# Causal linear attention on one core: a tile of 128 tokens worked as two chunks of 64 in divided TensorE arrays

## The reference

```python
q = (x @ Wq.T) -> 16 heads of 128;  k, v = (x @ Wk.T), (x @ Wv.T) -> 4 heads of 128
q, k = rope(q), rope(k);  qf, kf = elu(q) + 1, elu(k) + 1      # each k, v head serves 4 q heads
def step(carry, inp):                                          # once for each of 1024 tokens
    state = state + k_s[..., :, None] * v_s[..., None, :]
    z = z + k_s
    num = einsum('bhe,bhed->bhd', q_s, state)
    den = einsum('bhe,bhe->bh', q_s, z)[..., None] + 1e-6
    return (state, z), num / den
out = out.transpose(...) @ Wo.T
```

## Time and profile before

| what | value |
|---|---|
| median of three runs | 1032.81 us (1032.09 to 1033.21) |
| profiled execution, its own time | 1031.37 us |
| its span in the trace | 1029.6 us |
| PE busy over the span | 976.8 us (95%) |
| DVE, ACT, POOL busy | 681.7, 332.3, 249.5 us |
| TensorE's granted clock, mean | 0.995 of full |

### The profile page before, as it was taken

The page is one execution under the profiler, slowest core; times in us unless marked ns, Lnnn a source line. Parts: engine busy times, 40 slices in busy tenths (PEclk is TensorE's granted clock), DMA queues, the critical chain, the costliest instruction groups (busy, mean ns, idle before and its releaser), DMA issues. The chain is left out here.

```text
span 1029.6 us, 15693 instructions
## 1 busy us (share of the span) xinstructions
PE 976.8 (95%) x5994; PEld 791.1 (77%) x5994; DVE 681.7 (66%) x1494; ACT 332.3 (32%) x604; POOL 249.5 (24%) x320
## 2 busy tenths in 40 slices
PE   5899999999999999999978999998999999999997
PEld 4688888888888888888856788885666667778875
DVE  6766766666766667666565977765676776476556
ACT  4343333433333343334313323221122232422220
POOL 2232312222212323122201010023334554211011
PEclk9999999999999999999998999999999999999999
DMA  9400000000000000000004000002455340000000
GB/s 297 142 1 1 1 1 1 1 1 1 1 1 1 1 1 2 1 1 1 1 21 137 1 1 1 1 1 42 124 115 113 92 84 22 1 16 16 11 21 20
DMA packets 33051, 33.37 MB, mean 32 GB/s; under 512 B 6857, under 2 KB 26834, under 8 KB 32978
## 3 DMA queue, kind: packets, MB, share of 16 engines
q1 hardware_dynamic: 32978, 32.38, 11.9%
HBM read 23.98 MB, written 8.13 MB: 31 GB/s over the span
## 5 line engine op out<-in xcount | busy, mean ns | idle before, releaser
L396 POOL TENSOR_TENSOR rope_sum<-rope_cos,rope_sin 128x512 f32<-128x512 f32 x80 | 115.0, 1437 | 257.0 <-DVE rope_sin L517 257.0
L432 ACT ACTIVATE rope_exp<-rope_sum 128x512 f32<-128x512 f32 x80 | 50.5, 631 | 205.2 <-POOL rope_sum L396 205.1
L786 PE MATMUL proj<-wo_sb,attn_out_t 128*128 128x256 f32 x512 | 113.2, 379 | 0.7 <-issue 0.7
L786 PEld LDWEIGHTS proj<-wo_sb,attn_out_t 128*128 128x128 f32 x512 | 96.1, 190 | 13.4 <-issue 0.9
L735 PE MATMUL num<-v_ones,score_masked 128*128 128x129 f32 x512 | 99.2, 275 | 5.9 <-DVE score_masked L575 5.9
L736 PE MATMUL num<-state,q_t 128*128 128x129 f32 x512 | 99.0, 275 | 0.0
L2052 DVE SCALAR_TENSOR_TENSOR m_acc<-m_expert,gates,m_acc 128x256 f32<-128x256 f32 x128 | 61.9, 484 | 46.3 <-PE m_expert L2101 39.9
L735 PEld LDWEIGHTS num<-v_ones,score_masked 128*128 128x128 f32 x512 | 82.1, 191 | 13.4 <-DVE score_masked L575 8.0
L514 DVE TENSOR_TENSOR rope_cos<-proj,cos_sb 128x512 f32<-128x512 f32 x80 | 55.3, 691 | 52.3 <-PE proj L689 52.3
L689 PE MATMUL proj<-w_hi,a_h_hi 128*128 128x512 f32 x192 | 79.0, 493 | 4.1 <-DVE w_lo L139 2.4
L736 PEld LDWEIGHTS num<-state,q_t 128*128 128x128 f32 x512 | 77.7, 192 | 0.0
(11 more groups left out here) (250 smaller groups left out, 1883.6 us busy)
## 6 DMA issues: line engine op xcount, KB each, us to landing
kv_scratch<-t_kv SPq DMA_DIRECT2D x16, 256.0 KB, 2.4
kv_rows<-kv_scratch SPq DMA_DIRECT2D x32, 128.0 KB, 3.7
a_stage<-in_wqkv SPq DMA_DIRECT2D x6, 512.0 KB, 5.3
wo_sb<-in_wo SPq DMA_DIRECT2D x1, 2048.0 KB, 9.6
a_stage<-in_wgu SPq DMA_DIRECT2D x4, 512.0 KB, 9.7
out<-x_sb SPq DMA_DIRECT2D x16, 128.0 KB, 1.7
u_scratch<-u_rows SPq DMA_DIRECT2D x28, 64.0 KB, 2.9
t_u<-u_scratch SPq DMA_DIRECT2D x14, 128.0 KB, 2.2
```

Of the source, the lines that this page charges most:

```text
L396: pool.tensor_tensor(y[:, parity], t1[:, parity], t2[:, parity], ALU.add).then_inc(s["y_done"], 1)
L786: mm = pe.matmul(proj[:, b, 0:D], o_t[:, i, :], wo[:, i, :], start=(i == 0), stop=(i == H - 1))
```

## The change

The tile's 128 tokens become two sides of 64. On TensorE:

- `scores(g)` is now two products, one for each side: 64 tokens of k (64 columns of the array) with the four heads' q of the same side (256 columns streamed). The two write partitions 0 to 63 and 64 to 127 of one bank. Scores between the second side and the first are no longer made.
- `numerators(g)` has, for each of two values of j, four products of 64 x 64 masked scores with `[v | 1]` of their side, in four quarters of the array, then four of 64 columns of q with a state, in two halves of the array. The first side takes `state`, the second takes `mid`.
- `mid` is the state at the tile's middle: `sums(..., slice(0, HP))`, four products over the first 64 tokens, stands behind `turn4(0)`, and DVE adds it to `state` at the head of its step. `mid` lies in the buffer `g_xn`, and has that name in the rows.
- The sums over all 128 tokens at the step's end stay, but are left out in the last chunk (steps 14 and 15), where nothing reads the state any more.
- The mask and the masking on DVE cover 256 columns in place of 512; ACT's copies of q and of the output put the two sides apart and together again; GpSimd makes the mask in two halves.

```diff
+HP = P // 2
-            causal = sb("causal", [P, P])
+            causal = sb("causal", [P, HP])
-            k_t, q_t = sb("k_t", [P, KVH, P]), sb("q_t", [P, KVH, REP * P])
+            k_t, q_t = sb("k_t", [P, KVH, P]), sb("q_t", [P, KVH, 2, REP, HP])
+            mid = self.g_xn[:].rearrange("p i d -> p (i d)")[:, 0:KVH * VW].rearrange("p (g w) -> p g w", w=VW)
+            def num_item(c, b, j):
+                return at(c, b, KVH + 2, j) - (1 if last(c, b) else 0)
...
                     for g in range(KVH):
-                        drain_turn(c, b, 1 + g, q_t[:, g], turn[:, bank(1 + g), :])
+                        drain_turn(c, b, 1 + g, q_t[:, g].rearrange("p k r t -> p r k t"),
+                                   turn[:, bank(1 + g), :].rearrange("p (r k t) -> p r k t", r=REP, k=2))
...
                     def masked(g):
                         dve.wait_ge(s["score_full"], at(c, b, KVH, g + 1))
-                        dve.tensor_tensor(am[:, g % 2].rearrange("p (r t) -> p r t", r=REP),
-                                          score[:, g % 2, :].rearrange("p (r t) -> p r t", r=REP),
-                                          causal[:].unsqueeze(1).broadcast_to([P, REP, P]),
+                        dve.tensor_tensor(am[:, g % 2, 0:REP * HP].rearrange("p (r t) -> p r t", r=REP),
+                                          score[:, g % 2, 0:REP * HP].rearrange("p (r t) -> p r t", r=REP),
+                                          causal[:].unsqueeze(1).broadcast_to([P, REP, HP]),
                                           ALU.mult).then_inc(s["score_free"], 1)
+                    def state_of(item, dst):
+                        dve.wait_ge(s["num_full"], item + 1)
+                        dve.tensor_tensor(dst.rearrange("p (k h) w -> p k (h w)", k=2), num[:, :, 0:2 * VW],
+                                          state[:, b].rearrange("p (k h) w -> p k (h w)", k=2),
+                                          ALU.add).then_inc(s["num_free"], 1)
...
+                    state_of(num_item(c, b, 0), mid)
                     if nxt:
                         split(at(c, b, 1, 2), nb, 2 + 1 + at(c, b, 10, 1))
...
-                        pe.matmul(score[:, g % 2, :], k_t[:, g, :], q_t[:, g, :], start=True, stop=True
-                                  ).then_inc(s["score_full"], 1)
+                        for side in range(2):
+                            rows = slice(side * HP, (side + 1) * HP)
+                            mm = pe.matmul(score[rows, g % 2, 0:REP * HP], k_t[:, g, rows],
+                                           q_t[:, g, side].rearrange("p r t -> p (r t)"), start=True, stop=True)
+                        mm.then_inc(s["score_full"], 1)
                     def numerators(g):
                         pe.wait_ge(s["score_free"], 2 + at(c, b, KVH, g + 1))
-                        pe.wait_ge(s["num_free"], at(c, b, KVH + 1, g + 1))
-                        for r in range(REP):
-                            dst = num[:, r // 2, (r % 2) * VW:(r % 2 + 1) * VW]
-                            pe.matmul(dst, am[:, g % 2, r * P:(r + 1) * P], v[:, b, g, :], start=True, stop=False)
-                            mm = pe.matmul(dst, q_t[:, g, r * P:(r + 1) * P], state[:, b, g, :], start=False, stop=True)
+                        pe.wait_ge(s["num_free"], num_item(c, b, 1 + g) + 1)
+                        for j in range(2):
+                            places = [(side, q, num[q * HP:(q + 1) * HP, side, j * VW:(j + 1) * VW], 2 * j + q)
+                                      for side in range(2) for q in range(2)]
+                            for side, q, dst, r in places:
+                                rows = slice(side * HP, (side + 1) * HP)
+                                pe.matmul(dst, am[rows, g % 2, r * HP:(r + 1) * HP], v[rows, b, g, :], start=True, stop=False)
+                            for side, q, dst, r in places:
+                                mm = pe.matmul(dst, q_t[:, g, side, r, :], mid[:, g, :] if side else state[:, b, g, :],
+                                               start=False, stop=True)
                         mm.then_inc(s["num_full"], 1)
+                    def sums(item, rows):
+                        pe.wait_ge(s["num_free"], item + 1)
+                        for g in range(KVH):
+                            mm = pe.matmul(num[:, g // 2, (g % 2) * VW:(g % 2 + 1) * VW],
+                                           feat[rows, b, 0, g * P:(g + 1) * P], v[rows, b, g, :], start=True, stop=True)
+                        mm.then_inc(s["num_full"], 1)
...
                     turn4(0, feat[:, b, 0, :])
+                    sums(num_item(c, b, 0), slice(0, HP))
                     q_turn(0)
...
-                    pe.wait_ge(s["num_free"], at(c, b, KVH + 1, KVH + 1))
-                    for g in range(KVH):
-                        mm = pe.matmul(num[:, g // 2, (g % 2) * VW:(g % 2 + 1) * VW], feat[:, b, 0, g * P:(g + 1) * P],
-                                       v[:, b, g, :], start=True, stop=True)
-                    mm.then_inc(s["num_full"], 1)
+                    if c < NC - 1:
+                        sums(num_item(c, b, KVH + 1), slice(0, P))
                     out_turn(3)
```

More of the change, by code:

```diff
@@ L381, in _ @@
                 pool.wait_ge(s["mask_one"], 1)
-                pool.affine_select(out=causal[:], in_=causal[:], compare_op=ALU.is_ge, fill=0.0, base=0,
-                                   pattern=[[1, P]], channel_multiplier=-1).then_inc(s["causal_made"], 1)
+                for side in range(2):
+                    rows = causal[side * HP:(side + 1) * HP, :]
+                    pool.affine_select(out=rows, in_=rows, compare_op=ALU.is_ge, fill=0.0, base=0,
+                                       pattern=[[1, HP]], channel_multiplier=-1).then_inc(s["causal_made"], 1)
+                    pool.wait_ge(s["causal_made"], side + 1)
                 def rstd_of(n, b):
@@ L465, in step @@
                     for g in range(KVH):
-                        drain_turn(c, b, 5 + g, o_t[:, g * REP:(g + 1) * REP, :],
-                                   turn[:, bank(5 + g), :].rearrange("p (r t) -> p r t", r=REP))
+                        drain_turn(c, b, 5 + g, o_t[:, g * REP:(g + 1) * REP, :].rearrange("p r (k t) -> p k r t", k=2),
+                                   turn[:, bank(5 + g), :].rearrange("p (k r t) -> p k r t", k=2, r=REP))
                         if g < 2:
@@ L565, in _ @@
                 dve.memset(rden[:], 0.0).then_inc(s["num_free"], 1)
-                dve.wait_ge(s["causal_made"], 1)
+                dve.wait_ge(s["causal_made"], 2)
                 dve.wait_ge(s["x1_in"], 16)
@@ L644, in step @@
                     f(2)
-                    dve.wait_ge(s["num_full"], at(c, b, KVH + 1, KVH + 1))
-                    dve.tensor_tensor(state[:, b].rearrange("p (k h) w -> p k (h w)", k=2),
-                                      num[:, :, 0:2 * VW], state[:, b].rearrange("p (k h) w -> p k (h w)", k=2),
-                                      ALU.add).then_inc(s["num_free"], 1)
+                    if c < NC - 1:
+                        state_of(num_item(c, b, KVH + 1), state[:, b])
                     q_rope(4)
@@ L737, in numerators @@
+                        mm.then_inc(s["num_full"], 1)
[4 more added lines that the diff above has]
+                                           feat[rows, b, 0, g * P:(g + 1) * P], v[rows, b, g, :], start=True, stop=True)
                         mm.then_inc(s["num_full"], 1)
                     def out_turn(g):
-                        pe.wait_ge(s["num_free"], 1 + at(c, b, KVH + 1, g + 1))
+                        pe.wait_ge(s["num_free"], 2 + num_item(c, b, 1 + g))
```

2 lines of the change are left out of this document (1 added, 1 removed).

## The result

The changed kernel takes 1063.33 us in the median of 4 runs (1058.44 to 1066.12) against 1033.01 us for the kernel before: ratio 1.0287, 95% interval 1.0245 to 1.0330. The forecast was 1059 us, within 1036 to 1072, with a chance of 0.84 for slower.

The account below looks back on a forecast made before the run. TensorE's stream was taken as the bound; 4.7 + 13 x 1.6 + 0.7 - 0.4 = +25.8 us, taken as 26, on the profiled 1031.4 gave 1057.6, and 1059 us against the median, within 1036 to 1072.

Parts of the forecast that it names:

- What bounds the kernel: Steps 1 to 14: TensorE's stream is the bound, PE busy 445.21 of 450 us; shorter DVE work buys nothing.
- The overlap in parts of the array: Score and numerator blocks: products in different parts run together; quarters block 0.39 us, halves block 0.59 us, changes included.
- The price of a change of form: TensorE, 28 changes a step: 0.15 us into 64 columns or before transposes, 0.20 into the whole array; 4.3 us together.
- the twelve changes that no row showed: Changes between quarters and halves: between 0 and 0.15 us each, up to 1.8 a step; full price taken.
- The step: Regular step: 0.7 + 0.45 - 0.44 + 0.86 = +1.6 us, from numerators, leaving for transposes, scores and head.
- The head: Step's start up to the first projection `p(0)`: added sums and changes make it +0.86 us.
- T + 3.17: Kernel before: earliest start of `p(0)`, 3.17 us after the step's first transpose at T; T + 4.03 after the change.
- The rest of the step: Regular step outside its head: numerators +0.7, leaving for transposes +0.45, three score pairs -0.44 us; +0.7 together.
- The first step: Sums wait for the gates, `p(0)` moves from 40.04 to 44.05; +4.0, with the rest of the step 4.7 us.
- The last step: Step 15: dropped sums and hidden changes against 0.8 us added at the head; about -0.4 us.
- DVE's cover: Step 15: PE waits for DVE, 2.36 us at one place, which hides the changes of form.
- one restart: First step: PE restarts at 39.3 us behind the gates and runs slow for some 3 us.

Follow-up runs that it names:

- the merged blocks: Changed kernel with each numerator group's two blocks in quarters put together, then its two in halves: 1040.55 us, ratio 1.0052, step 31.77 us.
- scores alone: Kernel before with only the score products divided in halves and the mask over 256 columns, old numerators, no mid-tile sums: 1026.41 us, ratio 0.9933.
- the warmed kernel: Changed kernel with all five rearrangements, plus five unread products in the first step's idle stretch: 1021.95 us, repeated at 1022.54 us.
- e10_no_sums: Changed kernel without the head's sums of 64 tokens and DVE's add, both sides taking the tile's starting state: 1043.32 us, ratio 1.0109.
- the second profile: Changed kernel measured again, unaltered: 1061.61 us, ratio 1.0269, last step 34.05 us.
- e6_first_step: Changed kernel with, in the first step alone, the sums behind the third q transposes and DVE's add behind its split: 1056.22 us, ratio 1.0219.

## Why the prediction was right

- **What bounds the kernel.** Right: PE is the bound in the regular steps, its one wait is 3.5 us in all, and DVE's new work at the head costs nothing. ACT's rearranged copies cost no more either: it is busy for 332.3 us in both profiles.
- **The overlap in parts of the array.** Right for both forms: 0.38 and 0.59 for blocks forecast at 0.39 and 0.59. Rows of two other divisions, by columns alone and by rows alone, carried over to quarters.
- **The price of a change of form.** Right, 0.155 by the merged blocks against 0.15, and 0.35 for the two around the sums. The full price for the twelve changes that no row showed was a choice, argued from the nearest rows; eight of the twelve were then measured by the merged blocks. It decided which way the regular step went: without the twelve it would be 31.15, without the two around the sums as well 30.8, both shorter than before's 31.53. Here the trace agrees, by the price that it shows, with the Trainium skill, TensorEngine Tiling (Array Packing), section Tiling Modes, where it says that changing the mode drains the engine: also from quarters to halves, and from 64 to 128 rows.
- **The step.** Forecast +1.6, measured +1.48. The head is exact: from the first transposes to `p(0)` it was 3.09 before (the prediction's T + 3.17 was a little late) and is 208.76 to 212.71, 3.95, after: +0.86, as forecast. The rest of the step is +0.62 where +0.71 was forecast. The kernels that part the change give scores -0.45, numerators +0.90, sums +1.03; these can't be laid beside the prediction's terms one by one, since it counts the first score pair in the head and lets the second share its form with the numerators.
- **The first step.** The term was too small: 4.7 forecast, 8.2 measured. The mechanism, sums that wait for the gates, was right and its wait is in the rows. Off were two things. The gates came 1.85 us later (41.00 against 39.15 for the memset), as products ahead of them ran at half clock (the pair at 25.12 lasts 1.05, at full clock 0.63). This is no peculiarity of one execution: of the profiles of kernels with the sums at the head ten of eleven show it, those of the three kernels without them (before, scores alone, no state in mid tile) do not, though the work ahead of the gates is the same; and the two of the warmed kernel, one with and one without it, differ by 2.19 us in the memset and in the first product with wo. And half clock lasted until 48.7 and not for some 3 us from the restart at 41.1, which is the other 1.7 us. With the unread products in the idle stretch this second fall was gone in both profiles. Why the clock falls ahead of the gates, and why it stays down longer than at the restart of before, is not shown; it stayed down longer in the kernel without a state in mid tile too (e10_no_sums).
- **The last step.** Wrong in sign: -0.4 forecast, +3.7 measured. The sums that go and DVE's cover were right, as the kernels with a last step of 30.6 and 30.9 us show, 1 us less than before's, without anything changed in it but the order of scores in one of them. But a stretch of 17 us at half clock came with it, 13.6 in the second profile, which the prediction did not name.
- **Sum.** +25.8 against +33.3 on the profiled executions, +30.3 and +28.7 on the medians of the two measurements. The regular steps give 19.2 of the 33.3, forecast at 20.8 (13 x 1.6). All of the miss is in the ends: 3.5 us in the first step, 4.1 in the last, 1.6 behind it, each with more time at half clock than before. The prediction had put the clock in for one restart only.

## What to carry to other kernels

Count changes of the array's form before counting cells saved: a block of small products must save more stream than a change costs, here 0.16 to 0.18 us on average, and eight in a row share one. The same work lost 2.9% in one order. With products of one form put together, the sums moved into an existing wait and unread products in the last step it took 1022.54 against 1033.52 us, 1.2% less by the ratio of 0.9884; the regular step went from 33.01 to 30.78. Where a kernel idles at its start or end, its total also hangs on the clock that it comes back to, and a gain there has to be looked for again at the end.

## What was not expected of the hardware

- PE worked without a gap from 38.27 us and still ran at half clock until about 48 (first step of e6_first_step), while in the kernel before it was back at full pace by 40.04 after a restart at 36.60. With five whole-array products in the idle stretch the clock did not fall there, in both profiles of that kernel.
- Idle stretches of equal length, 2.36 and 2.38 us in the last step, were followed by full clock in the one profile of before and by half clock after the change, in both profiles of it and for 3.4 to 17.1 us in the others with divided products. Two unread products in each of two such stretches kept it full in four profiles out of four.
- Four float32 products in quarters of the array ran at once, each with its own weight load of 64 columns: two such blocks behind one change, sixteen records, took 0.60 us.
